# Linear attention on Trainium2: the softmax sums of the queries with the block matrix stationary, and a reciprocal of the whole tile

## The chip, the cores and the metric

The program runs on one core of one Trainium2 chip. The metric is the time on the device in microseconds (us); smaller is better. The kernel before took 1982.77 us as the median of three runs (1982.44 to 1983.53).

## The reference, cut to what matters

The program computes four residual blocks one after the other on `x` of shape (8, 256, 1024): a linear attention, a feed-forward network with 4-bit weights, an autocorrelation attention and a small linear layer. The change lies in the first. There the 256 tokens of a batch are the channels of eight heads of 32, and the 1024 features are the positions:

```python
def _L0_xattn_ref(q, k, v):            # q = layernorm(x), k = v = ctx, each (8, 256, 1024)
    qh = q.transpose(0, 2, 1).reshape(B, N, H, dh)      # H = 8, dh = 32
    ...
    qh = jax.nn.softmax(qh, axis=3)     # over the 32 rows of a head
    kh = jax.nn.softmax(kh, axis=1)     # over the 1024 positions
    kvs = jnp.einsum('bnhd,bnhe->bhde', kh, vh)
    out = jnp.einsum('bnhd,bhde->bnhe', qh, kvs)
    return out.transpose(0, 2, 3, 1).reshape(B, C, N)

x = x + jnp.tanh(g_xattn[0]) * _L0_xattn_ref(_layernorm(x, axis=-1), ctx_4096, ctx_4096)
```

So every exponential of a query is divided by the sum of the exponentials of the 32 rows of its head at the same position.

## The kernel before, in words

The attention works on 16 tiles (8 batches, two halves `h`) of 128 rows by 1024 columns of fp32. A tile holds four heads of 32 rows. `blk` is a 128x128 matrix of ones in four 32x32 blocks on the diagonal, `ident` the identity. All engines run the same loop of steps `i` = 0 to 18 (`run`), each with its own instructions of the step in the order in which they are written in its `step`; semaphores tie them together. There is no scheduler.

For tile i, step i does this:

- TensorE turns the keys' exponentials (`psE`, L488) and takes the queries' sums (`psB`, L494). Here a 128x128 piece of `eq` is stationary and `blk` moves, eight times, so the sums come out turned: a row of `psB` is a position, and each sum stands 32 times side by side.
- VectorE takes the reciprocal of every 32nd column (L562, 128x32). ScalarE writes each of the results 32 times into `rSx` (L454), TensorE turns `rSx` back into `psB` (L512, eight transposes), ScalarE copies that to `rSx` again (L461), and GpSimd multiplies `eq` by it (L401). TensorE uses the product in step i+1 (`psO`, L501).
- TensorE also makes the keys-by-values matrix (L507), which VectorE scales into `kvm` (L579).

In the same step VectorE adds the attention output of tile i-1 to `X` (L567), takes its statistics (L530, L533) and, when GpSimd has done the power -0.5 (L392, L394), the offset of the second layer norm (L538). Then it prepares tile i+2: statistics, maximum of the context (L545), and once more an offset that needs GpSimd's power (L538 again). L552 makes the low half of a turned output tile of step i-3, in steps 3 and later. ScalarE takes the exponentials of tile i+1 (L419, L425), normalizes output tile i-1 (L471), copies `ekT` (L448) and the high half (L430), and in steps 1 to 16 works on weights of the next block (L442).

The order on GpSimd in a step is: power for output tile i-1, multiplication of tile i (L401), power for tile i+2. The order on VectorE is that of its `step`:

```python
dve.wait_ge(sums_mm, i + 1)
dve.reciprocal(rS[h][:], psB[:, 0:D:ROWS0]).then_inc(rS_done, 1)
...
dve.wait_ge(out_mm, i)
dve.scalar_tensor_tensor(X[:, i - 1, :], psO[:], tg[:, 0:1], X[:, i - 1, :], ALU.mult, ALU.add).then_inc(x_done, 1)
...
offset(i - 1, 1 - h, mv2, rstd2, nmr2, rstd2_done, nmr2_done)
prepare(i + 2, h)
```

`rSx` exists once and `psB` once, `eq` twice. The feed-forward block (`phase_nf4_ffn`) starts when the attention has ended on all engines.

Of the kernel before, what the change touches and what calls it, by code (L numbers as in the profile page):

```python
# [26 lines left out]
P = 128  # L27
B, L, D = 8, 256, 1024
TILES = B * L // P
KD = D // P  # L30
# [255 lines left out]
def phase_linear_attention(nc, io, res):  # L286
# [9 lines left out]
    with ExitStack() as ctx:  # L296
# [7 lines left out]
        c_in, cT, eq, ek, ekT = (sb(n, [P, D]) for n in ("c_in", "cT", "eq", "ek", "ekT"))  # L304
        xn = [t.rearrange("p a b -> p (a b)") for t in (res["wt"][:, 2:4, :], res["absm"][:, 0:2, :])]
        spare = parts(res["made"][:].rearrange("p a b -> p (a b)").bitcast(F32))
        kvm, rS, st, st2 = ([spare(n) for h in range(2)] for n in (P, D // ROWS0, 12, 12))
        spare = parts(res["made"][:].rearrange("p a b -> p (a b)").bitcast(F32)[:, 4 * P - 48:])
        mv, mv2, ve, rstd, nmr, ve2, rstd2, nmr2, cm, ncm, ksum, rks = ([spare(n) for h in range(2)] for n in (2, 2, *(1,) * 10))
        rSx = res["wt"][:, 0:2, :].rearrange("p a b -> p (a b)")  # L310
# [6 lines left out]
        mv_done, rstd_done, nmr_done = (sem(n) for n in ("mv_done", "rstd_done", "nmr_done"))  # L317
        cmax_done, ncm_done, eq_done, ek_done, rks_done = (sem(n) for n in ("cmax_done", "ncm_done", "eq_done", "ek_done", "rks_done"))
        ekT_mm, ekT_done, kv_mm, kvm_done = (sem(n) for n in ("ekT_mm", "ekT_done", "kv_mm", "kvm_done"))
        sums_mm, rS_done, rSx_done, rS_mm, eqn_done, out_mm, x_done = (sem(n) for n in ("sums_mm", "rS_done", "rSx_done", "rS_mm", "eqn_done", "out_mm", "x_done"))  # L320
        mv2_done, rstd2_done, nmr2_done = (sem(n) for n in ("mv2_done", "rstd2_done", "nmr2_done"))
        turned_done = sem("turned_done")
        hi_done = res["hi_done"]
        xn_done, xT_mm, lo_done = (sem(n) for n in ("xn_done", "xT_mm", "lo_done"))

# [22 lines left out]
        with nc.Block() as block:  # L348
# [38 lines left out]
            @block.gpsimd  # L387
            def _(pool):
                def rsqrt(i, h, mv_, ve_, rs_, mvd, rsd):
                    pool.wait_ge(mvd, 3 * i + 3)  # L390
                    settle(pool)
                    pool.tensor_scalar(ve_[h][:], mv_[h][:, 1:2], EPS, None, ALU.add).then_inc(rsd, 1)  # L392
                    pool.wait_ge(rsd, 2 * i + 1)
                    pool.tensor_tensor(rs_[h][:], ve_[h][:], mhalf[:], ALU.pow).then_inc(rsd, 1)  # L394

                def step(i, h):
                    if exists(i - 1):
                        rsqrt(i - 1, 1 - h, mv2, ve2, rstd2, mv2_done, rstd2_done)
                    if exists(i):
                        pool.wait_ge(turned_done, i + 1)  # L400
                        pool.tensor_tensor(eq[h][:], rSx[:], eq[h][:], ALU.mult).then_inc(eqn_done, 1)  # L401
                    if exists(i + 2):
                        rsqrt(i + 2, h, mv, ve, rstd, mv_done, rstd_done)

                pool.memset(mhalf[:], -0.5).then_inc(const_set, 1)
                pool.memset(res["half"][:], 0.5).then_inc(const_set, 1)
                pool.memset(res["ones"][:], 1.0).then_inc(const_set, 1)
                pool.wait_ge(const_set, 3)
                for h in range(2):
                    rsqrt(h, h, mv, ve, rstd, mv_done, rstd_done)  # L410
                run(pool, step, scales_pool)

            @block.scalar
            def _(act):
                def query_exponentials(i, h):
                    act.wait_ge(nmr_done, i + 1)
                    after(act, out_mm, i - 1)
                    settle(act)
                    act.activation(eq[h][:], X[:, i, :], ACT.Exp, scale=rstd[h][:], bias=nmr[h][:]).then_inc(eq_done, 1)  # L419

                def key_exponentials(i, h):
                    after(act, ekT_mm, i - 1)
                    after(act, rks_done, i - 1)
                    act.wait_ge(ncm_done, i + 1)
                    act.activation(ek[h][:], c_in[h][:], ACT.Exp, bias=ncm[h][:], accum_out=ksum[h][:]).then_inc(ek_done, 1)  # L425

                def turned_high(i):
                    act.wait_ge(xT_mm, i + 1)
                    settle(act)
                    act.activation(halves_of(i, 0), turned_bank(), ACT.Copy, scale=LN_SCALE).then_inc(hi_done, 1)  # L430

                def first_kinks(i):

                    turn, k = divmod(i - 1, len(kinks))
                    if 0 <= turn < 2:
                        scale, bias, alpha = kinks[k]
                        act.wait_ge(res["first_in"], 16 * (AHEAD // 2) * (turn + 1))
                        if k:
                            act.wait_ge(res["kink_done"], AHEAD // 2 * (i - 1))
                        for u in range(AHEAD // 2 * turn, AHEAD // 2 * (turn + 1)):  # L440
                            block_u = res["first"][:, u, :]
                            act.activation(block_u, block_u if k else block_u.bitcast(I32), ACT.Prelu, bias=bias, scale=scale, alpha=alpha).then_inc(res["kink_done"], 1)  # L442

                def step(i, h):
                    if exists(i):
                        after(act, kv_mm, i - 1)
                        act.wait_ge(ekT_mm, i + 1)
                        act.activation(ekT[h][:], psE[:], ACT.Copy).then_inc(ekT_done, 1)  # L448
                    first_kinks(i)
                    if exists(i):  # L450
                        after(act, eqn_done, i)
                        act.wait_ge(rS_done, i + 1)

                        act.activation(rSx[:].rearrange("p (n r) -> p n r", r=ROWS0), rS[h][:].unsqueeze(2).to_broadcast([P, D // ROWS0, ROWS0]),  # L454
                                       ACT.Copy).then_inc(rSx_done, 1)
                    if exists(i + 1):
                        query_exponentials(i + 1, 1 - h)
                        key_exponentials(i + 1, 1 - h)
                    if exists(i):
                        act.wait_ge(rS_mm, i + 1)  # L460
                        act.activation(rSx[:], psB[:], ACT.Copy).then_inc(turned_done, 1)  # L461
                    if i == 0:
                        act.wait_ge(bound_in, 32)
                        act.activation(tg[:], gates[:], ACT.Tanh).then_inc(tanh_done, 1)
                    if i == TILES:
                        turned_high(i - 2)
                    if exists(i - 1):
                        after(act, xT_mm, i - 2)
                        act.wait_ge(nmr2_done, i)
                        settle(act)  # L470
                        act.activation(xn[1 - h][:], X[:, i - 1, :], ACT.Identity, scale=rstd2[1 - h][:], bias=nmr2[1 - h][:]).then_inc(xn_done, 1)  # L471
                    if exists(i - 2) and i != TILES:
                        turned_high(i - 2)

                act.wait_ge(const_set, 2)
                act.activation(rstd2[0][:], res["half"][:], ACT.Exp)
                key_exponentials(0, 0)
                query_exponentials(0, 0)
                run(act, step, scales_act)

            @block.tensor
            def _(pe):
                def step(i, h):
                    if exists(i):
                        after(pe, kvm_done, i)
                        pe.wait_ge(ek_done, i + 1)
                        for k in range(KD):
                            mm = pe.transpose(psE[:, k * P:(k + 1) * P], ek[h][:, k * P:(k + 1) * P], ident[:])  # L488
                        mm.then_inc(ekT_mm, 1)

                        after(pe, turned_done, i)
                        pe.wait_ge(eq_done, i + 1)
                        for k in range(KD):
                            mm = pe.matmul(psB[:, k * P:(k + 1) * P], eq[h][:, k * P:(k + 1) * P], blk[:], start=True, stop=True)  # L494
                        mm.then_inc(sums_mm, 1)
                    if exists(i - 1):
                        pe.wait_ge(eqn_done, i)
# [5 lines left out]
                    if exists(i):  # L503
                        pe.wait_ge(ekT_done, i + 1)
                        pe.wait_ge(cT_in[h], (i // 2) * 16 + 16 if isinstance(i, int) else (i - h) * 8 + 16)
                        for k in range(KD):
                            mm = pe.matmul(psE[:, 0:P], ekT[h][:, k * P:(k + 1) * P], cT[h][:, k * P:(k + 1) * P], start=(k == 0), stop=(k == KD - 1))  # L507
                        mm.then_inc(kv_mm, 1)

                        pe.wait_ge(rSx_done, i + 1)  # L510
                        for k in range(KD):
                            mm = pe.transpose(psB[:, k * P:(k + 1) * P], rSx[:, k * P:(k + 1) * P], ident[:])  # L512
                        mm.then_inc(rS_mm, 1)
                    if exists(i - 2):
                        pe.wait_ge(xn_done, i - 1)
                        after(pe, lo_done, i - 2)
# [8 lines left out]
            def _(dve):  # L525
# [28 lines left out]
                def step(i, h):  # L554
                    if exists(i - 3) and i != TILES + 1:
                        turned_low(i - 3)
                    if exists(i):
# [1 line left out]
                        dve.reciprocal(rks[h][:], ksum[h][:]).then_inc(rks_done, 1)  # L559
                        dve.wait_ge(sums_mm, i + 1)  # L560

                        dve.reciprocal(rS[h][:], psB[:, 0:D:ROWS0]).then_inc(rS_done, 1)  # L562
                    if exists(i - 1):
                        dve.wait_ge(out_mm, i)
                        if i == 1:
# [2232 lines left out]
```

## Time and profile before

| | |
|---|---|
| median of three runs | 1982.77 us (1982.44 to 1983.53) |
| profiled execution | 1984.28 us, its span 1982.5 us |
| TensorE (PE) busy | 1925.9 us, 97% of the span |
| VectorE (DVE) busy | 1268.0 us, 64% |
| ScalarE (ACT) busy | 1248.0 us, 63% |
| GpSimd (POOL) busy | 822.3 us, 41% |
| mean granted TensorE clock | 0.992 |
| chain that ended last | PE 21%, DVE 2%, issue 1% |

The profile is one execution; its time stands 1.5 us above the median, and the span is the part of it between the first and the last instruction. PE is TensorE's matmuls, PEld its weight loads, DVE is VectorE, ACT is ScalarE and POOL is GpSimd. A busy share is a mean over the four blocks, and these have different limits: the linear attention is about the first 176 us of the span.

### The profile page before, as it was taken

The page shows a single profiled execution, that of the slowest core. Times are in us where ns is not written, and L with a number is a line of the kernel's source. Part 1 is how long each engine was busy: PE and PEld are TensorE (multiplying, and loading weights), DVE is VectorE, ACT ScalarE, POOL GpSimd, SP SyncE. Part 2 cuts the span into 40 slices and gives each one's busy share as a digit, 9 for nine tenths or more (in the row PEclk, how much of TensorE's full clock was granted, in tenths as well). Part 3 has the DMA queues.
Part 4 walks back from the last instruction along what each step waited for, and adds up shares of the span by engine and source line. Part 5 has one row for each costly group of instructions (what it writes and reads, how often), then busy time and mean ns, then how long its engine had stood idle before and what let it go on. Part 6 is the DMA issues. An engine that isn't in the chain of part 4 may idle for free. (4 is left out here: it accounts for less than half of the span.)

```text
span 1982.5 us, 26463 instructions
## 1 busy us (share of the span) xinstructions
PE 1925.9 (97%) x9188; PEld 969.2 (49%) x9188; DVE 1268.0 (64%) x2184; ACT 1248.0 (63%) x1989; POOL 822.3 (41%) x746
## 2 busy tenths in 40 slices
PE   7996999999999999999999999999999899999998
PEld 6773444444444444444444444444444455555544
DVE  6776666573645747365463745546389888888872
ACT  6885888667876777676777767765534444344431
POOL 3433644532222232232322323222278667767742
PEclk9997999999999999999999999999999999999999
DMA  6641733248566383765737465562551110111001
GB/s 222 204 164 54 245 99 96 104 169 284 196 212 233 113 279 110 241 202 168 262 102 269 145 222 200 159 246 77 202 165 32 33 53 24 47 54 38 27 22 43
DMA packets 89972, 288.33 MB, mean 145 GB/s; under 512 B 11760, under 2 KB 16496, under 8 KB 72944
## 3 DMA queue, kind: packets, MB, share of 16 engines
q1 hardware_dynamic: 89840, 286.64, 42.8%
q8 instruction: 74, 1.21, 0.3%
q14 instruction: 58, 0.48, 0.1%
HBM read 259.33 MB, written 27.26 MB: 145 GB/s over the span
## 5 line engine op out<-in xcount | busy, mean ns | idle before, releaser
L1050 ACT ACTIVATE first<-first 128x512 f32<-128x512 f32 (+1 forms) x1024 | 635.9, 626 | 26.3 <-DVE wt L1459 1.8
L1284 POOL TENSOR_TENSOR gu<-wt,gu 128x512 f16<-128x512 f32 x86 | 102.5, 1192 | 389.5 <-ACT gu L1071 389.5
L1459 DVE SCALAR_TENSOR_TENSOR wt<-first,w_scale,absm 128x512 f32<-128x512 f32 x132 | 102.3, 775 | 237.8 <-ACT first L1050 237.3
L1806 PE MATMUL a_psQ<-z,gu 128*128 128x512 f16 x840 | 187.2, 379 | 0.0
L2409 PE MATMUL a_psL<-z,l_x 128*128 128x512 f16 x768 | 170.7, 379 | 1.0 <-DVE l_x L2511 0.8
L1806 PE MATMUL a_psC<-z,gu 128*128 128x512 f16 x660 | 151.3, 379 | 0.0
L1806 PE MATMUL a_psC<-z 128*128 128x512 f16 x612 | 140.4, 379 | 0.0
L1462 DVE SCALAR_TENSOR_TENSOR wt<-a_psE,lora_gain,wt 128x512 f32<-128x512 f32 x132 | 99.1, 751 | 54.0 <-PE a_psE L1764 26.9
L1806 PEld LDWEIGHTS a_psQ<-z,gu 128*128 128x128 f16 x840 | 82.2, 98 | 99.1
L1284 POOL TENSOR_TENSOR dn_lo<-wt,dn_hi 128x512 f16<-128x512 f32 x42 | 49.0, 1167 | 192.1 <-ACT dn_hi L1071 192.1
L1296 POOL TENSOR_TENSOR hid_lo<-z,hid_hi 128x512 f16<-128x512 f32 x68 | 80.6, 1199 | 109.7 <-ACT hid_hi L1112 109.6
L1071 ACT ACTIVATE gu<-wt 128x512 f16<-128x512 f32 x86 | 53.5, 622 | 105.1 <-DVE wt L1462 81.3
L2409 PEld LDWEIGHTS a_psL<-z,l_x 128*128 128x128 f16 x768 | 74.9, 98 | 89.0 <-issue 1.2
L1521 DVE SCALAR_TENSOR_TENSOR X<-a_psL,ffn_gain,X 128x512 f32<-128x512 f32 x132 | 95.3, 745 | 24.5 <-PE a_psL L1863 24.4
L1284 POOL TENSOR_TENSOR z<-wt,z 128x512 f16<-128x512 f32 x51 | 59.8, 1188 | 103.2 <-ACT z L1071 103.2
L1863 PE MATMUL a_psL<-dn_hi,hid_hi 128*128 128x512 f16 x268 | 101.6, 379 | 0.2 <-DVE X L1521 0.2
L1863 PE MATMUL a_psL<-dn_hi,hid_lo 128*128 128x512 f16 x268 | 101.5, 379 | 0.0
L1521 DVE SCALAR_TENSOR_TENSOR X<-a_psQ,ffn_gain,X 128x512 f32<-128x512 f32 x106 | 77.7, 746 | 36.6 <-PE a_psQ L1863 36.6
L1806 PEld LDWEIGHTS a_psC<-z,gu 128*128 128x128 f16 x660 | 63.8, 98 | 74.2
L1521 DVE SCALAR_TENSOR_TENSOR X<-a_psC,ffn_gain,X 128x512 f32<-128x512 f32 x108 | 78.8, 746 | 32.6 <-PE a_psC L1863 32.6
L1863 PE MATMUL a_psL<-dn_lo,hid_hi 128*128 128x512 f16 x254 | 96.2, 379 | 0.0
L1806 PEld LDWEIGHTS a_psC<-z 128*128 128x128 f16 x612 | 59.5, 98 | 70.5
(421 smaller groups left out, 4180.5 us busy)
## 6 DMA issues: line engine op xcount, KB each, us to landing
z<-x_parts SPq DMA_DIRECT2D x126, 1024.0 KB, 5.8
first<-in_codes SPq DMA_DIRECT2D x132, 256.0 KB, 3.1
absm<-in_absmax SPq DMA_DIRECT2D x264, 128.0 KB, 3.4
c_in<-in_ctx SPq DMA_DIRECT2D x16, 512.0 KB, 5.1
X<-in_x SPq DMA_DIRECT2D x16, 512.0 KB, 4.8
cT<-in_ctxT SPq DMA_DIRECT2D x16, 512.0 KB, 3.5
o_sp<-in_w SPq DMA_DIRECT2D x16, 512.0 KB, 4.4
z<-in_ctx SPq DMA_DIRECT2D x8, 1024.0 KB, 7.2
```

The costliest lines, as they stand in the source:

```text
L1050: act.activation(level[w % 2][:], codes[w % RING] if k == 0 else level[w % 2][:], ACT.Prelu, bias=bias, scale=scale, alpha=alpha).then_inc ...
L1071: act.activation(dest(c, name, 0), wt[slot(name)], ACT.Copy).then_inc(whi_done, 1)
L1284: pool.tensor_tensor(low, source, high, ALU.subtract).then_inc(wlo_done, 1)
L1296: pool.tensor_tensor(low, buf, high, ALU.subtract).then_inc(hidlo_done, 1)
L1459: dve.scalar_tensor_tensor(wt[at], source[:], w_scale[:, m:m + 1], absm[w % RING][:], ALU.mult, ALU.mult).then_inc(scaled, 1)
L1462: dve.scalar_tensor_tensor(wt[at], ps_lora[w % 2], lora_gain[:, m:m + 1], wt[at], ALU.mult, ALU.add).then_inc(wt_done, 1)
L1521: dve.scalar_tensor_tensor(dst, ps_ring[down_bank(j, n)], ffn_gain[:], dst, ALU.mult, ALU.add).then_inc(acc_done, 1)
L1806: mm = pe.matmul(out, w[:, k * P:(k + 1) * P], xx[:, k], start=first and q == 0, stop=q == 3 * KD // 2 - 1, skip_group_check=True)
L1863: mm = pe.matmul(ps_ring[down_bank(j, n)], hh[c][:, i * P:(i + 1) * P], w[c][:, hf * BANK:(hf + 1) * BANK], start=(q == 0), stop=(q == len ...
L2409: mm = pe.matmul(sum_bank(d, half), a[:, ks], w[:, k, half * CB:(half + 1) * CB], start=(q == 0), stop=(q == 3 * KD - 1))
```

## The change

The sums are now taken with `blk` stationary and `eq` moving, in two matmuls of 512 columns, so each sum stands at every row of its head and at its own position, as `eq` does. The reciprocal is taken of the whole tile, 128x1024, from `psB` into `rSx`. The widening copy L454, the transposes L512 and the copy L461 go, with their semaphores, and GpSimd's multiplication waits for the reciprocal. `psB` is free for the next tile's sums when the reciprocal has read it (before: when L461 had), and the reciprocal of tile i waits until GpSimd has multiplied by that of tile i-1, since `rSx` exists once.

```diff
-        kvm, rS, st, st2 = ([spare(n) for h in range(2)] for n in (P, D // ROWS0, 12, 12))
+        kvm, st, st2 = ([spare(n) for h in range(2)] for n in (P, 12, 12))
...
                     if exists(i):
-                        pool.wait_ge(turned_done, i + 1)
+                        pool.wait_ge(rS_done, i + 1)
                         pool.tensor_tensor(eq[h][:], rSx[:], eq[h][:], ALU.mult).then_inc(eqn_done, 1)
...
                     first_kinks(i)
-                    if exists(i):
-                        after(act, eqn_done, i)
-                        act.wait_ge(rS_done, i + 1)
-
-                        act.activation(rSx[:].rearrange("p (n r) -> p n r", r=ROWS0), rS[h][:].unsqueeze(2).to_broadcast([P, D // ROWS0, ROWS0]),
-                                       ACT.Copy).then_inc(rSx_done, 1)
                     if exists(i + 1):
                         query_exponentials(i + 1, 1 - h)
                         key_exponentials(i + 1, 1 - h)
-                    if exists(i):
-                        act.wait_ge(rS_mm, i + 1)
-                        act.activation(rSx[:], psB[:], ACT.Copy).then_inc(turned_done, 1)
...
-                        after(pe, turned_done, i)
+                        after(pe, rS_done, i)
                         pe.wait_ge(eq_done, i + 1)
-                        for k in range(KD):
-                            mm = pe.matmul(psB[:, k * P:(k + 1) * P], eq[h][:, k * P:(k + 1) * P], blk[:], start=True, stop=True)
+                        for n in range(2):
+                            mm = pe.matmul(psB[:, n * BANK:(n + 1) * BANK], blk[:], eq[h][:, n * BANK:(n + 1) * BANK], start=True, stop=True)
                         mm.then_inc(sums_mm, 1)
...
-                        pe.wait_ge(rSx_done, i + 1)
-                        for k in range(KD):
-                            mm = pe.transpose(psB[:, k * P:(k + 1) * P], rSx[:, k * P:(k + 1) * P], ident[:])
-                        mm.then_inc(rS_mm, 1)
...
                         dve.wait_ge(sums_mm, i + 1)
 
-                        dve.reciprocal(rS[h][:], psB[:, 0:D:ROWS0]).then_inc(rS_done, 1)
+                        after(dve, eqn_done, i)
+                        dve.reciprocal(rSx[:], psB[:]).then_inc(rS_done, 1)
```

No other line changes but for the line numbers. Two places show how the instructions stand now. On ScalarE, one step of the attention before (`wt` and `absm` are the places of `rSx` and the normalized output, `made` that of the small operands):

```order
L448 ACTIVATE ekT<-psE 128x1024
L442 ACTIVATE first<-first 128x512 x2
L454 ACTIVATE wt<-made 128x1024
L419 ACTIVATE eq<-X,made 128x1024
L425 ACTIVATE ek,made<-c_in,made 128x1024
L461 ACTIVATE wt<-psB 128x1024
L471 ACTIVATE absm<-X,made 128x1024
L430 ACTIVATE z<-psX 128x2x512
```

and the same step with the change:

```order
L447 ACTIVATE ekT<-psE 128x1024
L441 ACTIVATE first<-first 128x512 x2
L418 ACTIVATE eq<-X,made 128x1024
L424 ACTIVATE ek,made<-c_in,made 128x1024
L461 ACTIVATE absm<-X,made 128x1024
L429 ACTIVATE z<-psX 128x2x512
```

The two copies into `wt` are gone; the exponentials no longer stand between two of ScalarE's parts of the sums' way.

On GpSimd, from the multiplication of one step to that of the next, before, with what each waits for:

```order
L401 TENSOR_TENSOR eq<-wt,eq 128x1024 [waits turned_done]
L392 TENSOR_SCALAR made<-made 128x1 [waits mv_done]
L394 TENSOR_TENSOR made<-made,mhalf 128x1 [waits rstd_done]
L392 TENSOR_SCALAR made<-made 128x1 [waits mv2_done]
L394 TENSOR_TENSOR made<-made,mhalf 128x1 [waits rstd2_done]
L401 TENSOR_TENSOR eq<-wt,eq 128x1024 [waits turned_done]
```

and with the change:

```order
L400 TENSOR_TENSOR eq<-wt,eq 128x1024 [waits rS_done]
L391 TENSOR_SCALAR made<-made 128x1 [waits mv_done]
L393 TENSOR_TENSOR made<-made,mhalf 128x1 [waits rstd_done]
L391 TENSOR_SCALAR made<-made 128x1 [waits mv2_done]
L393 TENSOR_TENSOR made<-made,mhalf 128x1 [waits rstd2_done]
L400 TENSOR_TENSOR eq<-wt,eq 128x1024 [waits rS_done]
```

The order is the same and the multiplication's wait is another: for VectorE's reciprocal, which VectorE does ahead of the statistics (`mv2_done`) that the powers before the multiplication wait for, and no longer for ScalarE's second copy.

## Rows read from the trace of the kernel before

**Rows 1.** Stretches: length; PE, PEld, DVE, ACT, POOL busy us; clock, DMA share, GB/s

```profile
42.93:52.26 9.33, 8.54 (x63) 7.07 (x62) 7.24 (x17) 8.27 (x10) 3.92 (x5) 1.00 0.62 226
...
188.70:200.00 11.30, 11.30 (x61) 5.38 (x60) 5.26 (x6) 7.60 (x12) 5.25 (x5) 0.99 0.18 55
```

**Rows 2.** Timeline of one step: start, duration, engine, line, output<-inputs, idle before

```profile
42.93 0.34 DVE L562 RECIPROCAL made<-psB 128x32 f32<-128x32 f32 x1
43.19 1.19 DVE L567 SCALAR_TENSOR_TENSOR X<-psO,tg,X 128x1024 f32<-128x1024 f32 x1
43.37 1.06 ACT L454 ACTIVATE wt<-made 128x1024 f32<-128x1024 f32 x1 [1.03 <-DVE made L562]
...
46.59 1.00 ACT L461 ACTIVATE wt<-psB 128x1024 f32<-128x1024 f32 x1
...
47.26 0.16 DVE L538 SCALAR_TENSOR_TENSOR made<-made 128x1 f32<-128x1 f32 x1 [0.84 <-POOL made L394]
...
47.68 2.37 POOL L401 TENSOR_TENSOR eq<-wt,eq 128x1024 f32<-128x1024 f32 x1 [0.45 <-ACT wt L461]
...
50.92 0.16 DVE L538 SCALAR_TENSOR_TENSOR made<-made 128x1 f32<-128x1 f32 x1 [0.81 <-POOL made L394]
...
51.06 1.21 DVE L552 SCALAR_TENSOR_TENSOR z<-psX,z 128x1024 f16<-128x1024 f32 x1
...
52.26 0.34 DVE L562 RECIPROCAL made<-psB 128x32 f32<-128x32 f32 x1
```

**Rows 3.** The timeline at the first two and the last two reciprocals and behind

```profile
15.15 0.36 DVE L562 RECIPROCAL made<-psB 128x32 f32<-128x32 f32 x1 [0.92 <-PE psB L494]
...
19.85 2.35 POOL L401 TENSOR_TENSOR eq<-wt,eq 128x1024 f32<-128x1024 f32 x1 [5.95 <-ACT wt L461]
...
23.29 0.34 DVE L562 RECIPROCAL made<-psB 128x32 f32<-128x32 f32 x1
...
145.46 0.34 DVE L562 RECIPROCAL made<-psB 128x32 f32<-128x32 f32 x1
...
153.45 0.34 DVE L562 RECIPROCAL made<-psB 128x32 f32<-128x32 f32 x1
...
154.63 1.28 DVE L567 SCALAR_TENSOR_TENSOR X<-psO,tg,X 128x1024 f32<-128x1024 f32 x1 [0.84 <-PE psO L501]
...
159.75 2.36 POOL L401 TENSOR_TENSOR eq<-wt,eq 128x1024 f32<-128x1024 f32 x1 [0.97 <-ACT wt L461]
```

**Rows 4.** The timeline of VectorE and GpSimd in the second step, 24 to 34

```profile
24.28 1.28 DVE L567 SCALAR_TENSOR_TENSOR X<-psO,tg,X 128x1024 f32<-128x1024 f32 x1 [0.65 <-PE psO L501]
...
28.39 2.35 POOL L401 TENSOR_TENSOR eq<-wt,eq 128x1024 f32<-128x1024 f32 x1
28.46 2.30 DVE L538 SCALAR_TENSOR_TENSOR made<-made 128x1 f32<-128x1 f32 x1 [0.85 <-POOL made L394]
...
33.41 0.16 DVE L538 SCALAR_TENSOR_TENSOR made<-made 128x1 f32<-128x1 f32 x1
...
33.62 0.34 DVE L562 RECIPROCAL made<-psB 128x32 f32<-128x32 f32 x1
```

**Rows 5.** VectorE's reciprocals by size: busy us, mean ns of one | idle before

```profile
L562 DVE RECIPROCAL made<-psB 128x32 f32<-128x32 f32 x16 | 5.4, 340 | 0.9 <-PE psB L494 0.9
L2573 DVE RECIPROCAL rws<-wsum 128x4 f32<-128x4 f32 x15 | 2.7, 178 | 0.5
L559 DVE RECIPROCAL made<-made 128x1 f32<-128x1 f32 x16 | 2.5, 154 | 0.0
```

**Rows 6.** TensorE's timeline, and the stretch that holds the row at 162.16

```profile
11.44 3.67 PE L494 MATMUL psB<-blk,eq 128*128 128x128 f32 x16 [2.31 <-ACT eq L419]
...
19.91 1.97 PE L494 MATMUL psB<-blk,eq 128*128 128x128 f32 x16
...
162.16 3.40 PE L501 MATMUL psO<-eq,made 128*128 128x512 f32 x4 [2.68 <-POOL eq L401]
...
162.10:165.40 3.30, 3.24 (x4) 1.40 (x5) 1.21 (x2) 0.65 (x2) 0.01 (x1) 0.55 0.00 0
```

More of the change, by code:

```diff
@@ L319, in phase_linear_attention @@
         ekT_mm, ekT_done, kv_mm, kvm_done = (sem(n) for n in ("ekT_mm", "ekT_done", "kv_mm", "kvm_done"))
-        sums_mm, rS_done, rSx_done, rS_mm, eqn_done, out_mm, x_done = (sem(n) for n in ("sums_mm", "rS_done", "rSx_done", "rS_mm", "eqn_done", "out_mm", "x_done"))
+        sums_mm, rS_done, eqn_done, out_mm, x_done = (sem(n) for n in ("sums_mm", "rS_done", "eqn_done", "out_mm", "x_done"))
         mv2_done, rstd2_done, nmr2_done = (sem(n) for n in ("mv2_done", "rstd2_done", "nmr2_done"))
-        turned_done = sem("turned_done")
         hi_done = res["hi_done"]
```

## The prediction

> **What bounds the kernel now.** I read first the busy time of each engine in a stretch, to see which engine is full where. In the feed-forward stage TensorE is busy in all of the 11.30 us from 188.7, while in one step of the linear attention, 42.93 to 52.26, it is busy for 8.54 of 9.33 us, ScalarE for 8.27 and VectorE for 7.24 [rows 1]. No engine is full there, so a ring of waits sets the step, and the change touches this stage alone.
>
> Second comes the timeline of one step, where the reader should follow the ring [rows 2]: VectorE's narrow reciprocal L562 at 42.93 releases ScalarE's widening copy L454 (waited 1.03); the query and key exponentials follow, then the copy L461 at 46.59; that releases GpSimd's multiplication L401 at 47.68 (2.37 long, waited 0.45). Behind the multiplication on GpSimd stands the rsqrt for tile i+2, which VectorE awaits in its second L538 of the step, at 50.92 (0.81 idle; the first, at 47.26, awaits the rsqrt of the output tile); then L552 and the next reciprocal at 52.26. From the start of L567 at 43.19 to that reciprocal are 9.07 us. VectorE lacks 0.81 us at this wait, ScalarE and TensorE are waited for earlier: VectorE with its two trips to GpSimd is nearly as long as the ring.
>
> Third, the places of the 16 reciprocals [rows 3, 4]: 15.15, 23.29, 33.62, then twelve intervals of 9.32 to 145.46, then 153.45; L567 of the last tile but one follows at 154.63, the last multiplication at 159.75. The program behind that is fed by this stage, so what is added here shifts the end by as much.
>
> **What the change takes away.** From ScalarE the copies L454 (1.06) and L461 (1.00), from TensorE eight transposes a step, about half of the sixteen passes that take 1.97 [rows 2, 6]. The sums themselves cost the same: two fp32 matmuls of 512 columns are four passes, as for L501, whose four at half clock took 3.40 where the sixteen small ones took 3.67. Sixteen steps of two copies are 33 us of ScalarE's time, but worth only what the ring's ScalarE part costs: the 0.45 us for which the multiplication waited. VectorE's own path allows no more.
>
> **What it adds: the reciprocal.** The reciprocal grows from 128x32 to 128x1024, still from PSUM. No row has that size. One column takes 154 ns, four take 178, thirty-two take 340 [rows 5]. From 1 to 32 columns the slope is 186/31 = 6.0 ns an element; from 1 to 4 it is 24/3 = 8.0. The bound from below is a 1024-element pass from PSUM at ordinary speed: L552, 1.21 us [rows 2]. I take 6.0, since 32 columns is the largest size and the very operand: 992 more elements are 5.95 us more on VectorE, a tile. The lower bound adds 0.87 us, 8.0 ns adds 7.9. Against the lower bound: at 1 ns an element thirty-two columns could not cost 186 ns more than one.
>
> The Trainium skill, "VectorE: DVE Perf Modes", section "The DVE is not a fixed-function vector unit", says that Reciprocal is an iterated divide with a repeat count of 8. Read as eight cycles of the page's 0.96 GHz an element, an estimate of 8.3 ns, that would be 8.3 us more a tile (992 x 8.3 ns), and a kernel of some 2129 us; the row of 32 columns speaks for less.
>
> **What it moves: the multiplication runs into L538.** GpSimd's order stays: rsqrt of the output tile, multiplication, rsqrt of tile i+2. The multiplication now waits for the reciprocal alone, which is over long before VectorE's statistics let GpSimd do the first rsqrt. So it starts straight behind that rsqrt, and so does VectorE's first L538, which waits for the same rsqrt. The trace has one step in which this happened: the multiplication starts at 28.39, L538 at 28.46 and takes 2.30 us, not 0.16 [rows 4, 2]; it ends with the multiplication. In all other steps the 0.45 us of waiting for L461 let L538 pass first. From L567 (24.28) to the next reciprocal (33.62) that step has 9.34 us without the L552 of later steps; with it (50.92 to 52.26 against 33.41 to 33.62, so 1.13 more) 10.47, against 9.07: +1.40.
>
> The Trainium skill, "SBUF — State Buffer", section "Who interferes with whom", says that a VectorE instruction with two SBUF inputs and a GpSimd instruction that reads SBUF exclude each other for the whole instruction, in order of issue. L538 has two such inputs and the row at 28.46 agrees; by that rule L567 and L579, with one input in PSUM, stay free, and the price falls on L538 in every step.
>
> **The sum.**
> - Reciprocal 0 to 1: what follows it on VectorE is 5.95 late, but at 23.29 VectorE was waiting on GpSimd's multiplication. Now this starts at about 21.5 instead of 19.85: +1.7. TensorE has stood idle meanwhile; transposes and sums at half clock (2.0 and 3.67) after 22 end near 27.7: +4.4. I take +3.5.
> - 1 to 2: the stop is already in it, and L567 started 0.99 after the reciprocal where now 6.2 passes: +5.2.
> - Twelve intervals at 5.95 + 1.40 = 7.35: +88.2.
> - 14 to 15: no preparation of another tile lies behind L538 to soak up any of the 2.1: 5.95 + 2.1 = +8.0.
> - Tail: L567 starts 6.2 after 153.45, 5.0 later than 154.63, and the multiplication saves its wait of about 1 us for L461 (it stood at 159.75): +4.1.
>
> That is +109.0 us. The profiled execution took 1984.28 (span 1982.5), so 2093.3; the median of the runs, 1982.77, is 1.5 lower, which makes it 2091.8: **2092**. Elsewhere nothing moves: the step becomes 16.7 us, the DMA loads are requested later by as much as their consumers come later; the kink activations on ScalarE lie in its new slack. TensorE's 8.54 us become about 7.5, which even at half clock, 15, fit into 16.7.
>
> **Rivals.**
> - *Eight ns an element.* For: the slope from one to four columns. Against: 340 ns at thirty-two. 16 x 1.98 = 32 more: 2124. Chance 0.14.
> - *TensorE's clock.* It will stand idle for 6 us and more of each step. At 162.16, after a wait, four passes took 3.40 us at a granted 0.55, that is mostly at 1.2 GHz [rows 6]. If everything ran so and its waits for GpSimd came on top of 15, the step would be a microsecond longer, twelve times: 2104. Chance 0.07.
> - *L538 slips ahead.* Then the step is 9.33 - 0.45 + 5.95: 5.5 more instead of 7.35, and 14 to 15 has 2.1 less: 2092 - 24 = 2068. Against: the one step with this order shows the stop. Chance 0.07.
> - *The reciprocal streams* (+0.87). Then the stop decides: 12 x 2.27 = 27, +3.0 for 14 to 15, about -1 in the tail, and -2.5 at the first interval, where the multiplication no longer waits: 2009. The 154 to 340 ns could come from the stride of 32 columns in PSUM. Chance 0.10.
> - *The ring only gets shorter,* the other side. ScalarE's links drop out of the ring from reciprocal to L538. If VectorE's share grew by less than 0.45 us a step and L538 were not stopped, each step would be shorter; with an unchanged reciprocal, 12 x 0.45, 2.5 and 1 less: 1974. It decides from below 0.45 us more, half of the streaming bound, and needs L538 in front as well. Chance 0.02.
>
> **How the numbers follow.** The forecast has 0.60. The range, 2060 to 2130, holds it, L538 slipping ahead, the clock and the eight nanoseconds, 0.88 together, less a little for errors of size; it leaves out the streaming reciprocal and the faster case. It is wide since 1 ns an element is 16 us. What a measurement here can tell from no change is about 0.2%, 4 us. Only the last rival is faster (0.02); 0.01 for none; slower 0.97.
>
> **What will show it.** The new reciprocal at 6.3 us, 16 times; steps of 16.7; L538 beside the multiplication at 2.3 us in fourteen or fifteen steps; ScalarE waiting on VectorE instead of the reverse; the feed-forward stage as long as now. A reciprocal under 2 us, or steps under 14 or over 18.5 us, would refute the sum.

## The result, and the profile after

The changed kernel takes 2097.13 us (median of four runs, 2095.52 to 2098.8) against 1982.61 (four runs, 1981.21 to 1983.53): the ratio is 1.0578, 95% interval 1.056 to 1.0597. It is 114.5 us slower, and 2092 had been forecast.

The page of the profiled execution, its header and the busy times:

```profile
span 2093.5 us, 25791 instructions
## 1 busy us (share of the span) xinstructions
PE 1935.6 (92%) x8868; PEld 955.8 (46%) x8868; DVE 1398.1 (67%) x2184; ACT 1217.9 (58%) x1957; POOL 821.8 (39%) x746
```

ScalarE lost 30.1 us of work and VectorE gained 130.1. Two groups of VectorE in the attention stage (0 to 291 us) carry that:

```profile
L549 DVE RECIPROCAL wt<-psB 128x1024 f32<-128x1024 f32 x16 | 104.6, 6540 | 3.2 <-PE psB L484 3.2
...
L524 DVE SCALAR_TENSOR_TENSOR made<-made 128x1 f32<-128x1 f32 x32 | 37.2, 1162 | 14.6 <-POOL made L393 14.3
```

The reciprocal takes 6.54 us, where 128x32 took 0.34 [rows 5]. L524 (L538 before) is the offset: 32 instructions of a single column, with 37.2 us of busy time where there were 7.2; 15 of the 32 take about 2.3 us. One step of the stage, where the columns are those of [rows 1]:

```profile
150.91:167.74 16.83, 9.15 (x40) 6.09 (x40) 15.53 (x17) 6.36 (x8) 3.89 (x5) 0.80 0.30 92
```

VectorE is now busy for 15.53 of 16.83 us and ScalarE for 6.36. TensorE stands still for almost half of the step; its granted clock is 0.80 on average. The timeline of the same step:

```profile
144.46 6.54 DVE L549 RECIPROCAL wt<-psB 128x1024 f32<-128x1024 f32 x1
150.91 1.19 DVE L554 SCALAR_TENSOR_TENSOR X<-psO,tg,X 128x1024 f32<-128x1024 f32 x1
...
154.20 1.97 PE L478 MATMUL psE<-ident,ek 128*128 128x128 f32 x8 [7.59 <-DVE made L566]
...
154.92 2.35 POOL L400 TENSOR_TENSOR eq<-wt,eq 128x1024 f32<-128x1024 f32 x1
154.99 2.30 DVE L524 SCALAR_TENSOR_TENSOR made<-made 128x1 f32<-128x1 f32 x1 [0.84 <-POOL made L393]
155.96 2.75 PE L484 MATMUL psB<-eq,blk 128*128 128x512 f32 x4
...
159.94 0.16 DVE L524 SCALAR_TENSOR_TENSOR made<-made 128x1 f32<-128x1 f32 x1
...
161.28 6.54 DVE L549 RECIPROCAL wt<-psB 128x1024 f32<-128x1024 f32 x1
```

From L554 at 150.91 to the next reciprocal are 10.37 us, where there were 9.07 [rows 2]; with the 6.45 us from the reciprocal's start to L554 the step is 16.82. What [rows 4] showed once is there each time: the multiplication starts at 154.92, L524 at 154.99, and both end together. The text calls this the stop. TensorE's eight transposes take 1.97 after a wait of 7.59, but the sums end at 158.7, well before 161.28.

The reciprocals that do not stand at this distance, and what follows the last one:

```profile
15.62 6.56 DVE L549 RECIPROCAL wt<-psB 128x1024 f32<-128x1024 f32 x1 [1.13 <-PE psB L484]
...
22.40 1.97 PE L478 MATMUL psE<-ident,ek 128*128 128x128 f32 x8 [3.94 <-DVE made L566]
...
24.16 3.62 PE L484 MATMUL psB<-eq,blk 128*128 128x512 f32 x4
...
27.82 6.56 DVE L549 RECIPROCAL wt<-psB 128x1024 f32<-128x1024 f32 x1 [2.05 <-PE psB L484]
...
43.52 6.54 DVE L549 RECIPROCAL wt<-psB 128x1024 f32<-128x1024 f32 x1
...
245.38 6.54 DVE L549 RECIPROCAL wt<-psB 128x1024 f32<-128x1024 f32 x1
...
261.71 6.54 DVE L549 RECIPROCAL wt<-psB 128x1024 f32<-128x1024 f32 x1
...
268.16 1.18 DVE L554 SCALAR_TENSOR_TENSOR X<-psO,tg,X 128x1024 f32<-128x1024 f32 x1
...
272.17 2.34 POOL L400 TENSOR_TENSOR eq<-wt,eq 128x1024 f32<-128x1024 f32 x1
272.24 2.29 DVE L524 SCALAR_TENSOR_TENSOR made<-made 128x1 f32<-128x1 f32 x1 [0.84 <-POOL made L393]
...
281.51 0.28 DVE L230 TENSOR_REDUCE absm<-psB 9x1 f32<-9x128 f32 x1 [1.46 <-PE psB L212]
...
294.49 1.01 PE L1755 MATMUL a_psE<-lora_b,lora_a 96*128 96x128 f16 x8 [6.27 <-DVE lora_a L1645]
```

The last row is the first matmul of the feed-forward stage, before the change at

```profile
179.62 1.01 PE L1768 MATMUL a_psE<-lora_b,lora_a 96*128 96x128 f16 x8 [6.40 <-DVE lora_a L1658]
```

Against the places of [rows 3], the forecast and the measured price of each interval between reciprocals are:

| interval | before | after | forecast | measured |
|---|---|---|---|---|
| start to reciprocal 0 | 15.15 | 15.62 | 0 | +0.5 |
| 0 to 1 | 8.14 | 12.20 | +3.5 | +4.1 |
| 1 to 2 | 10.33 | 15.70 | +5.2 | +5.4 |
| twelve steps | 12 x 9.32 | 12 x 16.82 | +88.2 | +90.0 |
| 14 to 15 | 7.99 | 16.33 | +8.0 | +8.3 |
| 15 to the feed-forward | 26.17 | 32.78 | +4.1 | +6.6 |
| sum | | | +109.0 | +114.9 |

The first 0.5 is not the change's: in two runs below whose code is the same up to this reciprocal (free, two_in) it starts at 14.64 and 14.76. From the first reciprocal to the feed-forward are 164.47 us before and 278.87 after, 114.4 more.

The span grew by only 111.0 us. The 3.9 us between this and the table's 114.9 lie in the stages behind, whose code is the same: from the first feed-forward matmul to the end are 1802.9 us before and 1799.0 after. What differs there is TensorE's granted clock at a few places. These are the first 10 us of that part and 20 us that begin 1300 us into it, before and then after:

```profile
179.62:189.62 10.00, 7.26 (x31) 3.45 (x32) 6.36 (x7) 1.26 (x2) 2.95 (x2) 0.53 0.59 172
...
1479.62:1499.62 20.00, 17.23 (x65) 7.86 (x64) 16.95 (x35) 10.37 (x18) 16.71 (x15) 0.83 0.28 90
```

```profile
294.49:304.49 10.00, 7.52 (x38) 3.67 (x39) 7.82 (x9) 1.89 (x3) 3.38 (x3) 0.67 0.55 171
...
1594.49:1614.49 20.00, 15.20 (x68) 7.93 (x67) 17.79 (x30) 9.36 (x14) 18.93 (x16) 1.00 0.22 67
```

In the 20 us that begin 1360 us into it the clock is 0.91 before and 1.00 after; in 20 us stretches over the whole part there is no other difference above 0.01 but in the last 3 us. The twelve profiled executions of this study divide by the two stretches from 1300 and 1360 us on: the six with less than 1.00 in one or both of them (before, copy, before_swap, before_swap_free, late, two_in) take 1801.7 to 1802.9 us for the part, the other six 1798.8 to 1799.6. Forms of both kernels stand on either side. What brings the lower clock about is open.

So, in what follows, the step and the start of the feed-forward stage are the sharper readings, and a difference of 4 us between two spans proves nothing about the attention.

### The profile page after: what moved, and what is told of

It reads as the page before. It is cut to its first block and busy times, and to the rows that moved or that the text cites. A ratio compares the mean times of both kernels' runs of the same rounds, so it can differ in the third digit from the quotient of the medians.

```text
span 2093.5 us, 25791 instructions
## 1 busy us (share of the span) xinstructions
PE 1935.6 (92%) x8868; PEld 955.8 (46%) x8868; DVE 1398.1 (67%) x2184; ACT 1217.9 (58%) x1957; POOL 821.8 (39%) x746
## 5 line engine op out<-in xcount | busy, mean ns | idle before, releaser
L478 PE MATMUL psE<-ident,ek 128*128 128x128 f32 x128 | 31.5, 427 | 112.5 <-DVE made L566 105.0
L549 DVE RECIPROCAL wt<-psB 128x1024 f32<-128x1024 f32 x16 | 104.6, 6540 | 3.2 <-PE psB L484 3.2
```

The source lines that it names most:

```text
L549: dve.reciprocal(rSx[:], psB[:]).then_inc(rS_done, 1)
```

## The experiments

In the order in which they ran; "step" is the distance from one L567 (L554 in the forms of the changed kernel) to the next, and "feed-forward at" the start of its first matmul, both in the profiled execution. Each ratio is to runs of the kernel before that were made beside that run, so it can differ from the quotient of the medians by some 0.0005.

| run | median us | ratio to before (95%) | step us | feed-forward at |
|---|---|---|---|---|
| before | 1982.61 | | 9.32 | 179.62 |
| after | 2097.13 | 1.0578 (1.056 to 1.0597) | 16.82 | 294.49 |
| copy | 2012.85 | 1.0151 (1.0134 to 1.0168) | 11.57 | 209.45 |
| free | 2072.02 | 1.0446 (1.0431 to 1.0462) | 15.08 to 15.18 | 267.75 |
| copy_free | 1984.15 | 1.001 (1.0001 to 1.002) | 9.85 | 183.68 |
| before_sums | 1982.88 | 0.9997 (0.9988 to 1.0007) | 9.32 | 180.01 |
| before_swap | 2003.84 | 1.0105 (1.009 to 1.0121) | 10.63 | 201.87 |
| before_swap_free | 1987.07 | 1.0024 (1.0015 to 1.0033) | 9.56 | 183.13 |
| before_free | 1980.27 | 0.999 (0.9981 to 0.9999) | 9.37 | 179.75 |
| late | 1990.6 | 1.0041 (1.0028 to 1.0054) | 8.91 and 10.71 by turns | 188.62 |
| late_free | 1975.11 | 0.9962 (0.9949 to 0.9974) | 8.61 and 8.90 by turns | 173.06 |
| two_in | 2096.54 | 1.0574 (1.0543 to 1.0605) | 16.82 | 293.65 |

### The reciprocal: a copy in its place

```diff
-                        dve.reciprocal(rSx[:], psB[:]).then_inc(rS_done, 1)
+                        dve.tensor_copy(rSx[:], psB[:]).then_inc(rS_done, 1)
```

> The changed kernel with a plain copy of psB into rSx in place of the reciprocal, so the division by the sums is left out (GpSimd multiplies by the sums). Theory (the reciprocal costs 6 cycles an element, and that is most of the loss): the instruction falls from 6.54 us to about 1.2 us, the step from 16.82 to about 11.5 us, the time from 2097 to about 2010 us, still above the kernel before, since L524 beside the multiplication is still stopped for 2.3 us. Rival (the 128x1024 pass is slow because of its source in PSUM or its size, not because of the division): the copy takes 5 us or more and the time stays above 2080 us.

VectorE's group in this kernel:

```profile
L549 DVE COPY wt<-psB 128x1024 f32<-128x1024 f32 x16 | 19.3, 1208 | 0.8 <-PE psB L484 0.8
```

The same tile from the same place in PSUM passes in 1.21 us, and the time falls to 2012.85, where 2010 was expected. So 5.33 of the 6.54 us are the division; sixteen times that is 85.3 us, and the time fell by 84.3. Neither the size nor PSUM makes it slow, and since this read has a stride of one, the stride of the narrow reciprocal is not the reason either: from 340 ns at 32 columns to 6540 at 1024 are 6.25 ns an element.

### The stop: another form of the offset

```diff
-                    dve.scalar_tensor_tensor(nm_[h][:], mv_[h][:, 0:1], -1.0, rs_[h][:], ALU.mult, ALU.mult).then_inc(nmd, 1)
+                    dve.tensor_scalar(nm_[h][:], mv_[h][:, 0:1], rs_[h][:], -1.0, ALU.mult, ALU.mult).then_inc(nmd, 1)
```

> The changed kernel with the offset of the layer norm (L524) written as a tensor_scalar, whose only SBUF tensor is the mean and which takes the power as its per-partition scalar; the same numbers. Theory (L524 is stopped because it has two SBUF inputs while GpSimd's multiplication reads SBUF): L524 takes 0.16 us everywhere, the step falls from 16.82 to about 15.0 us, the time from 2097 to about 2070 us. Rival (VectorE is held up by GpSimd's program whatever the instruction's form, or the wait is for the power to become visible): L524 still takes 2.3 us, and the time stays at 2097 us.

Two rows of its timeline, a multiplication and the offset beside it:

```profile
125.95 2.36 POOL L400 TENSOR_TENSOR eq<-wt,eq 128x1024 f32<-128x1024 f32 x1
126.02 0.21 DVE L524 TENSOR_SCALAR made<-made 128x1 f32<-128x1 f32 x1 [0.85 <-POOL made L393]
```

With the power as a per-partition scalar instead of a second tensor the offset passes in 0.21 us beside the running multiplication. None of the 32 is over 1 us. The time is 2072.02, 25 us less than the changed kernel: that is the stop's whole price there, and one line mends it. A step is 1.7 us shorter. That is more than the 1.30 by which the step's path grew above: there the stop also took the place of a wait of 0.81 us, here only of one of 0.33.

Whether the fused form or its two SBUF inputs are to blame, this edit does not tell. The last run does; it leaves out the factor -1:

```diff
-                    dve.scalar_tensor_tensor(nm_[h][:], mv_[h][:, 0:1], -1.0, rs_[h][:], ALU.mult, ALU.mult).then_inc(nmd, 1)
+                    dve.tensor_tensor(nm_[h][:], mv_[h][:, 0:1], rs_[h][:], ALU.mult).then_inc(nmd, 1)
```

> The changed kernel with the offset (L524) as a tensor_tensor product of mean and power, so another instruction with the same two SBUF inputs; the factor -1 is left out. Theory (two inputs in SBUF decide, not the instruction's form): L524 is stopped for 2.3 us beside each multiplication, as in the changed kernel, the step stays 16.82 us, and the time stays at 2097 us, give or take 3. Rival (the fused form scalar_tensor_tensor alone is stopped): L524 takes 0.2 us, the step is 15.1 us, and the time is that of the tensor_scalar version, 2072 us.

```profile
137.25 2.35 POOL L400 TENSOR_TENSOR eq<-wt,eq 128x1024 f32<-128x1024 f32 x1
137.31 2.30 DVE L524 TENSOR_TENSOR made<-made 128x1 f32<-128x1 f32 x1 [0.85 <-POOL made L393]
```

Another instruction with the same two inputs is stopped in 15 places as before, step and time unchanged. The inputs decide, which is what the rule of the Trainium skill ("SBUF — State Buffer", "Who interferes with whom") says; the rows show besides that one column per partition is enough.

### Both taken away: what the removed copies and transposes were worth

> Both edits at once: the changed kernel with a plain copy in place of the reciprocal (the division is left out) and with the offset as a tensor_scalar. Theory (a ring of VectorE and GpSimd sets the step, and the ScalarE copies and TensorE transposes that the change removed were worth 0.45 us of it at most): the step is about 9.75 us against 9.33 before, the time 1984 us, 0 to 5 us above the kernel before. Rival (the removed copies and transposes were on the path with their whole 3 us): about 8 us a step or less, and 1960 us or less.

It has the edits of copy and of free. 1984.15 us: without the division's price and without the stop, a kernel that lacks ScalarE's 33 us of copies and eight transposes a step is no faster than the one before. It lies 113.0 us below the changed kernel; the two edits alone gave 84.3 and 25.1, so they add up to within 3.6 us. Its step is 9.85, VectorE's path:

```profile
79.53 1.21 DVE L549 COPY wt<-psB 128x1024 f32<-128x1024 f32 x1
...
84.75 2.36 POOL L400 TENSOR_TENSOR eq<-wt,eq 128x1024 f32<-128x1024 f32 x1
84.82 0.21 DVE L524 TENSOR_SCALAR made<-made 128x1 f32<-128x1 f32 x1 [0.85 <-POOL made L393]
...
87.99 0.21 DVE L524 TENSOR_SCALAR made<-made 128x1 f32<-128x1 f32 x1 [0.32 <-POOL made L393]
...
89.38 1.21 DVE L549 COPY wt<-psB 128x1024 f32<-128x1024 f32 x1
```

The second wait for GpSimd fell from 0.81 [rows 2] to 0.32: this is the removal's worth, 0.49 us a step. It is the multiplication's own gain: it starts 0.07 us ahead of the first offset, where it started 0.42 behind [rows 2]. The wider pass takes it back, as it is 0.87 us longer.

### The sums alone

```diff
-                        for k in range(KD):
-                            mm = pe.matmul(psB[:, k * P:(k + 1) * P], eq[h][:, k * P:(k + 1) * P], blk[:], start=True, stop=True)
+                        for n in range(2):
+                            mm = pe.matmul(psB[:, n * BANK:(n + 1) * BANK], blk[:], eq[h][:, n * BANK:(n + 1) * BANK], start=True, stop=True)
```

> The kernel before with the sums alone taken the new way, two matmuls of 512 columns with the block matrix stationary; the rest stays, so the values that the narrow reciprocal reads are other sums than the right ones. Theory (four passes of 512 columns cost what sixteen of 128 cost, and TensorE is not waited for here): the sums take 1.9 to 2.0 us as before and the time is within 2 us of 1982.6. Rival (the new form is cheaper or dearer by itself): the sums differ by more than 0.3 us and the time by more than 3 us.

```profile
L501 PE MATMUL psO<-eq,made 128*128 128x512 f32 x64 | 32.3, 628 | 9.4 <-POOL eq L401 9.4
L494 PE MATMUL psB<-eq,blk 128*128 128x512 f32 x64 | 32.3, 628 | 2.3 <-ACT eq L419 2.3
```

and the sums in the kernel before:

```profile
L494 PE MATMUL psB<-blk,eq 128*128 128x128 f32 x256 | 33.2, 285 | 2.3 <-ACT eq L419 2.3
```

1982.88 us, interval 0.9988 to 1.0007: no difference. The sums take 32.3 us in all where they took 33.2, and cost as much as the output matmuls of the same shape. This part of the change is free.

### The stop put into the kernel before

ScalarE's turned copy is put ahead of the key exponential, so the multiplication no longer waits for it:

```diff
                     if exists(i + 1):
                         query_exponentials(i + 1, 1 - h)
-                        key_exponentials(i + 1, 1 - h)
                     if exists(i):
                         act.wait_ge(rS_mm, i + 1)
                         act.activation(rSx[:], psB[:], ACT.Copy).then_inc(turned_done, 1)
+                    if exists(i + 1):
+                        key_exponentials(i + 1, 1 - h)
```

> The kernel before with ScalarE's turned copy (L461) put ahead of the key exponential of the next tile, so that GpSimd's multiplication no longer waits 0.45 us for it and starts straight behind the first power, beside L538. Nothing else changes. Theory (L538, with two SBUF inputs, is stopped by the multiplication whenever it comes second, and that costs 1.4 us a step): L538 takes 2.3 us in all steps, the step grows from 9.33 to about 10.5 us, and the time is about 2000 us, although ScalarE delivers sooner. Rival (the stop of the second step had another cause, or costs nothing where it falls): the step is 8.9 to 9.3 us and the time 1975 to 1983 us.

```profile
83.21 2.36 POOL L401 TENSOR_TENSOR eq<-wt,eq 128x1024 f32<-128x1024 f32 x1
83.28 2.31 DVE L539 SCALAR_TENSOR_TENSOR made<-made 128x1 f32<-128x1 f32 x1 [0.84 <-POOL made L394]
```

Delivering the multiplication's input 0.45 us sooner makes the kernel 21 us slower: 14 offsets are stopped where one was, and the step is 10.63. This separates the stop from the long reciprocal. The next run, the same order without the stop, shows how much of the 21 us is the stop's: 16.8; the rest is the order's.

> The same with the offset (L538) as a tensor_scalar. Theory: no stop, and the ring shorter by the 0.45 us of waiting: the step is about 8.9 us and the time 1973 to 1978 us, below the kernel before. Rival (the key exponential, now a copy later, or VectorE's own path takes the place of the wait): the step stays at 9.3 us and the time within 3 us of 1982.6.

It came out the other way: 1987.07 us, slower than before, step 9.56. The rows of one step:

```profile
84.62 1.02 ACT L460 ACTIVATE wt<-psB 128x1024 f32<-128x1024 f32 x1 [0.85 <-PE psB L513]
...
85.55 1.14 ACT L425 ACTIVATE ek<-c_in,made 128x1024 f32<-128x1024 f32 x1
...
86.92 1.06 PE L489 MATMUL psE<-ident,ek 128*128 128x128 f32 x8 [1.46 <-ACT ek L425]
...
91.53 1.28 DVE L568 SCALAR_TENSOR_TENSOR X<-psO,tg,X 128x1024 f32<-128x1024 f32 x1 [0.47 <-PE psO L502]
```

ScalarE now waits 0.85 us for the turning that the key exponential used to cover, the exponential comes later, TensorE waits 1.46 us for it, and its output matmuls, next in its order, keep VectorE's L568 waiting 0.47. The rival had named this cause, but its numbers, 9.3 us and within 3 us of 1982.6, were missed as well.

> The kernel before with only the offset (L538) as a tensor_scalar. Theory (before, the stop fell on one step alone, the second): the step stays 9.33 us, and the time falls by 1 to 2 us, to about 1981. Rival (the form itself is faster or slower in all 32 places): a difference of more than 4 us.

1980.27 us, interval 0.9981 to 0.9999. Its one stop is gone and the interval between two L567 that held it fell from 9.60 to 8.55, but the step is 9.37, as the offset takes 0.21 us instead of 0.16, and the feed-forward begins at 179.75, not sooner. So the attention won next to nothing. The profiled execution has a granted clock of 1.00 at the two later places named above, where that of the kernel before has 0.83 and 0.91, and its stages behind the attention are 3.8 us shorter. Among the runs with a mean granted clock of 0.995 the medians are 1981.29 before and 1980.27 here, so about 1 of the 2 us goes with the clock; the rest stays unexplained.

### A version that beats both

If the ring of [rows 2] sets the step, it can be cut where it touches VectorE: the second offset of a step is first read behind the next reciprocal.

```diff
-                    offset(i, h, mv, rstd, nmr, rstd_done, nmr_done)
+                    if i == 1 and isinstance(i, int):
+                        offset(i, h, mv, rstd, nmr, rstd_done, nmr_done)
...
                         dve.reciprocal(rS[h][:], psB[:, 0:D:ROWS0]).then_inc(rS_done, 1)
+                    if exists(i + 1) and (not isinstance(i, int) or i > 0):
+                        offset(i + 1, 1 - h, mv, rstd, nmr, rstd_done, nmr_done)
```

> The kernel before with VectorE's offset of tile i+2 (the second L538 of a step, which waited 0.81 us for GpSimd) moved behind the next step's narrow reciprocal; its first reader, the query exponential, stands behind that reciprocal anyway. Theory (the ring reciprocal, ScalarE, multiplication, power, L538, reciprocal sets the step of the kernel before): it is cut here, VectorE stands ready 0.8 us sooner, and the next tie is the multiplication, the output matmuls and L567, some 8.9 to 9.1 us; the time falls by 3 to 6 us, to 1977 to 1979. Rival (ScalarE with 8.27 us of work and its own waits holds the step, or L538 falls beside the multiplication): 9.3 us a step or more and 1982 us or more.

Missed: 1990.6 us. Steps of 8.91, the ones hoped for, take turns with 10.71, and each long one has a stopped offset:

```profile
114.77 2.34 POOL L401 TENSOR_TENSOR eq<-wt,eq 128x1024 f32<-128x1024 f32 x1
114.80 2.33 DVE L538 SCALAR_TENSOR_TENSOR made<-made 128x1 f32<-128x1 f32 x1 [0.84 <-POOL made L394]
```

A short step makes VectorE early against ScalarE, the multiplication then stands ready behind the power, and the offset, which starts 0.03 us behind it, is stopped. In the short steps the multiplication still waits 0.34 us for ScalarE and starts 0.31 behind the offset.

> The kernel before with both: the second offset behind the next narrow reciprocal, and the offsets as tensor_scalar. With the first edit alone some steps took 8.91 us and others longer, the long ones with the first L538 of the step stopped for over 2 us beside the multiplication. Theory (once VectorE gains on ScalarE, the multiplication stands ready behind the power and stops L538; without the stop the ring is short): every step takes 8.9 to 9.1 us, and the time is 1976 to 1980 us, below the kernel before. Rival (the long steps come from ScalarE or TensorE, not from the stop): steps keep alternating and the time stays near 1990 us.

```profile
90.31 2.37 POOL L401 TENSOR_TENSOR eq<-wt,eq 128x1024 f32<-128x1024 f32 x1
90.31 0.21 DVE L538 TENSOR_SCALAR made<-made 128x1 f32<-128x1 f32 x1 [0.86 <-POOL made L394]
...
94.54 0.34 DVE L563 RECIPROCAL made<-psB 128x32 f32<-128x32 f32 x1
...
94.79 0.11 DVE L538 TENSOR_SCALAR made<-made 128x1 f32<-128x1 f32 x1
```

No stop, steps of 8.61 and 8.90, the feed-forward 6.6 us sooner than before, and 1975.11 us: ratio 0.9962 (0.9949 to 0.9974) to the kernel before. Both are a little better than expected (8.9 to 9.1, 1976 to 1980); that the steps still alternate had been said by the rival, though without the stop the two kinds differ by 0.3 us and not by 1.8. Neither edit does that alone.

## Why the prediction was right

- **What bounds the kernel.** A ring with slack on no engine but little of it on VectorE was the reading, and it held: copy_free shows that the links taken from ScalarE and TensorE were worth 0.49 us a step where 0.45 were forecast, and late_free shows that VectorE's second wait was the tie.
- **The reciprocal.** Taken at 6.0 ns an element, 6.2 us of VectorE, it measured 6.25 ns and 6.45 us. The term is short by 0.25 us, sixteen times 4 us. The slope from 1 to 32 columns was the better guide; the 8.0 from one to four columns is refuted by the row. So is the estimate of 8.3 ns that was worked out from the Trainium skill, "VectorE: DVE Perf Modes", section "The DVE is not a fixed-function vector unit", by reading its repeat count of 8 as cycles. At the 0.96 GHz of the Trainium skill, "VectorE: DVE Perf Modes", section "Specifications", 6.25 ns would be six cycles, an estimate.
- **The stop.** Forecast in every step at +1.40; it fell on 15 offsets, and the path from L567 to the reciprocal grew from 9.07 to 10.37, +1.30. It was read from a single row of the trace before, and free, two_in and before_swap show it as a cause of its own. Both numbers are net: the offset takes 2.14 us longer, and the second wait for GpSimd, 0.81 us, is gone.
- **The first interval.** +3.5 had been taken between 1.7 and 4.4; it was +4.1, with TensorE's transposes and sums taking 1.97 and 3.62 at a granted clock of 0.50, and VectorE waiting 2.05 us for them. The 3.67 us at 11.44 [rows 6], from which the half clock was inferred, stand in a stretch that the profile shows at 1.00; the inference held here all the same.
- **The tail** is the term that was mis-sized most: +4.1 forecast, +6.6 measured. The multiplication did come 4.2 us later, as said. But the stop was counted as costing nothing there, and it delays all that VectorE does behind it; by its last wait, for TensorE's L212, it is still 1.66 us behind free (L230 starts 13.35 us after L554, there 11.69). From L554 at 268.16 to the feed-forward are 26.33 us; in free, without the stop, 24.75 (243.00 to 267.75); before, 24.99. So the stop is 1.6 of the 2.5 us. Most of the rest is the wait for L461 that the multiplication was to save: counted as about 1 us, it shows as 0.24 (24.99 against 24.75).
- **TensorE's clock** in the steps: as forecast, slower work and no wait; VectorE never waited for the sums after the second reciprocal, 3.2 us in all being those of the first two.
- **The rivals.** The streaming reciprocal was priced at 2009 and its stand-in measured 2012.85; "L538 slips ahead" at 2068, and free measured 2072.02. That the removed work alone makes a faster kernel needs less than about 0.5 us more on VectorE, which copy_free (0.87 more, 1984.15) bears out from the other side. No run tried the case itself, a removal with an unchanged reciprocal.
- **The sum.** The terms were 5.4 us too small in all, 109.0 where the attention grew by 114.4 from its first reciprocal on, and the median stands 5.3 above the 2091.8 of the sum. So no error was made good by another; that the profiled execution, 2095.52, lies nearer to the forecast is owed to its later stages, 3.9 us shorter than before.

## What to carry to other kernels

Price an operation by its cost per element on its own engine before counting what it frees elsewhere: a reciprocal on one column in 32 with a copy, a turning and a copy behind it cost 9.32 us a step, the direct one 16.82, or 15.1 without the stop. Work that is removed is worth the wait that it ended, here 0.49 us of 3. When a wait goes, look at which instructions will now run side by side: between VectorE and GpSimd a one-column instruction with two SBUF tensors was worth 25 us, and writing one of them as a per-partition scalar removed that.

## What the runs showed of the hardware that was not expected

- The stop is a matter of 0.03 to 0.07 us, by which the multiplication starts ahead of the offset: in the kernel "late" it came and went in alternate steps with no change in the program, and shortening a step brought it on.
- A tensor_scalar of one fp32 column from SBUF to SBUF ran in 0.21 us beside GpSimd's multiplication and also without it, 0.05 longer than the form that is stopped takes when it is alone.
- The stages behind the attention, the same code each time, took 1798.8 to 1802.9 us in the profiled executions. The granted clock in their first 10 us lay between 0.51 and 0.68, and the six that took over 1801 us are those in which it fell below 1.00 once more in the 20 us that begin 1300 or 1360 us later.
